# Four 5-tap recurrences on one core: both batches in one 512-column matmul, with lines and bias put into PSUM first

## What is computed

```python
def step(w, b):
    def f(carry, inp):
        nxt = inp + _conv1d(carry, w, b)     # 5 taps, 48 -> 48 channels, bias b
        return (nxt, nxt)
    return f
_, d_rest = lax.scan(step(down_w, down_b), d0, xs[1:])
...
_, u_rest = lax.scan(step(down_w, down_b), u0, seq)
...
_, r_rest = lax.scan(step(right_w, right_b), r0, ws[1:])
...
_, l_rest = lax.scan(step(left_w, left_b), l0, R[Ww - 2::-1])
```

## Time and profile before

| what | value |
|---|---|
| median of 3 runs | 10235.59 us |
| lowest, highest | 10228.61, 10245.71 us |
| span of the profiled execution | 10244.7 us |
| TensorE / VectorE / ScalarE / GpSimd busy in that span | 90% / 75% / 61% / 29% |
| the four ways, from the first hi matmul to the last | about 5097 to 9500 us of the span |

### The profile page before, as it was taken

The page is one execution under the profiler, slowest core; times in us unless marked ns, Lnnn a source line. Parts: engine busy times, 40 slices in busy tenths (PEclk is TensorE's granted clock), DMA queues, the critical chain, the costliest instruction groups (busy, mean ns, idle before and its releaser), DMA issues. The chain is left out here.

```text
span 10244.7 us, 212155 instructions
## 1 busy us (share of the span) xinstructions
PE 9248.3 (90%) x72264; PEld 8910.2 (87%) x72264; DVE 7669.6 (75%) x15539; ACT 6283.6 (61%) x11050; POOL 2991.7 (29%) x4335
## 2 busy tenths in 40 slices
PE   3999999999999999999899999999999999999100
PEld 3999999999999997777699999999999999999100
DVE  8888888777777775666677777777899987777323
ACT  3777777777777775444466668999633346666000
POOL 0000000000000000000166666666666666666000
PEclk9999999999999999999899999999999999999555
DMA  8888887666666666999889896777766657777999
GB/s 269 168 170 168 168 170 143 131 129 133 136 131 135 135 131 150 291 278 293 235 191 195 203 195 191 219 210 217 210 205 217 211 184 200 196 203 188 370 433 401
DMA packets 770603, 2101.31 MB, mean 205 GB/s; under 512 B 58976, under 2 KB 633728, under 8 KB 674256
## 3 DMA queue, kind: packets, MB, share of 16 engines
q1 hardware_dynamic: 629824, 1744.21, 66.6%
q0 software_dynamic: 34304, 151.01, 5.7%
q10 hardware_dynamic: 106368, 204.76, 5.6%
HBM read 1344.55 MB, written 754.97 MB: 205 GB/s over the span
## 5 line engine op out<-in xcount | busy, mean ns | idle before, releaser
L1542 ACT CAST hi<-rough 112x256 fp32r<-112x256 f32 x4096 | 1666.2, 407 | 1414.4 <-DVE rough L1455 1362.8
L1375 PE MATMUL scan_ps<-hi,scan_high 112*112 112x256 f32 x12264 | 2122.7, 282 | 30.7 <-ACT hi L1542 30.7
L1455 DVE SCALAR_TENSOR_TENSOR rough<-scan_ps,scan_bias,lines 112x256 f32<-112x256 f32 x4086 | 2136.4, 523 | 18.4 <-issue 14.0
L1386 PE MATMUL scan_ps_low<-lo,scan_high 112*112 112x256 f32 x12264 | 2136.1, 283 | 0.9 <-POOL lo L1487 0.7
L1381 PE MATMUL scan_ps_low<-hi,scan_low 112*112 112x256 f32 x12264 | 2123.9, 282 | 0.0
L463 PE MATMUL conv_ps<-tap_low,x_high 128*128 128x432 f32 (+2 forms) x6144 | 1905.4, 310 | 0.0
L463 PE MATMUL conv_ps<-tap_high,x_low 128*128 128x432 f32 (+2 forms) x6144 | 1904.0, 310 | 0.0
L463 PE MATMUL conv_ps<-tap_high,x_high 128*128 128x432 f32 (+2 forms) x6144 | 1882.0, 306 | 11.7 <-DVE x_edge L659 7.3
L1375 PEld LDWEIGHTS scan_ps<-hi,scan_high 112*112 112x112 f32 x12264 | 1695.0, 176 | 32.0 <-ACT hi L1542 31.5
L1386 PEld LDWEIGHTS scan_ps_low<-lo,scan_high 112*112 112x112 f32 x12264 | 1685.7, 176 | 6.3 <-POOL lo L1487 2.1
L1381 PEld LDWEIGHTS scan_ps_low<-hi,scan_low 112*112 112x112 f32 x12264 | 1684.1, 176 | 0.0
(11 more groups left out here) (142 smaller groups left out, 11625.5 us busy)
## 6 DMA issues: line engine op xcount, KB each, us to landing
raw<-x SPq DMA_DIRECT2D x764, 256.0 KB, 5.0
d_rows<-lines SPq DMA_DIRECT2D x32, 3584.0 KB, 30.4
u_cols<-lines SPq DMA_DIRECT2D x64, 1792.0 KB, 13.3
r_cols<-lines SPq DMA_DIRECT2D x32, 3584.0 KB, 24.3
lines<-u_cols SPq DMA_DIRECT2D x31, 3584.0 KB, 16.5
lines<-r_cols SPq DMA_DIRECT2D x30, 3584.0 KB, 16.6
lines<-d_rows SPq DMA_DIRECT2D x30, 3360.0 KB, 15.7
v_blocks<-xs ACTq DMA_DIRECT2D x128, 768.0 KB, 4.5
```

Source lines behind the costliest of these rows:

```text
L1375: last = nc.tensor.matmul(ps[:, b, 0:LP], high[:, shift], hi[:, b, (k - 1) % 2, shift:shift + LP], start=shift == 0, stop=shift == 2)
L1386: last = nc.tensor.matmul(ps_low[:, b, 0:LP], high[:, shift], lo[:, b, shift:shift + LP], start=False, stop=shift == 2)
L1455: nc.vector.scalar_tensor_tensor(rough[:, b, k % 2], ps[:, b, 0:LP], bias, line(way, s, k % T, b, kept), ALU.add, ALU.add).then_inc(rough_ ...
L1542: nc.scalar.copy(hi[:, b, k % 2, 1:LP + 1], rough[:, b, k % 2]).then_inc(hi_ready[b], 1)
```

## The change

Both batches go through one step together: every matmul, cast, subtraction and addition covers 2 x 256 columns. PSUM has four slots of one bank each, `ps[:, k % 4]`; a slot is first filled with the line of step k plus the bias ("seed"), and all nine products of step k are then added to it (`start=False`). `hi` is the slot rounded after the high products, `lo` = the full slot - `hi` (now on VectorE), and the state = `hi` + `lo` (now on GpSimd). The seeds are made by ScalarE in the down and right ways, with the normalisation folded in for down, and by VectorE in the up and left ways; each is issued `AHEAD` = 2 steps ahead, behind the step's own work of that engine. The separate normalisation and `rough` are gone. `hi` has 4 buffers and `lo` 2. ScalarE's copies of the ring come 2 steps later than before (`LAG`). SyncE's waits go by the count of seeds and states in place of `rough` and states.

TensorE issues the high products of step k+1 ahead of the low products of step k. The core of the diff:

```diff
+    LAG = 2
+    AHEAD = 2
+    HIS, LOS, SLOTS = 4, 2, 4
...
+        ps, gn_ps = psum("scan_ps"), ctx.enter_context(nc.psum_tensor("gn1_ps", [PP, 2, B], F32))
...
+        def slot_free(engine, way, g, k, kept):
+            if not (way == "down" and kept and k < SLOTS):
+                engine.wait_ge(lo_ready, states0(way) + T * g + k - SLOTS + 1)
+
+        def high_free(engine, way, g, k, first):
+            if not (way == "down" and first and k < HIS):
+                engine.wait_ge(state_done, states0(way) + T * g + k - HIS + 1)
...
 SyncE
-                    for b in range(B):
-                        sp.wait_ge(rough_ready[b], states0(way) + T * g - T)
+                    sp.wait_ge(seeded[way], seeds0(way) + T * g - T)
...
 TensorE
+                def high_products(way, g, k):
+                    pe.wait_ge(seeded[way], seeds0(way) + T * g + k + 1)
+                    pe.wait_ge(hi_ready, states0(way) + T * g + k)
+                    for shift in range(3):
+                        last = nc.tensor.matmul(slot(k), w_hi[:, TAPS_OF[way], shift], hi[:, (k - 1) % HIS, :, shift:shift + LP],
+                                                start=False, stop=False, skip_group_check=True)
+                    last.then_inc(conv_done, 1)
+
+                def low_products(way, g, k):
+                    pe.wait_ge(hi_ready, states0(way) + T * g + k + 1)
+                    for shift in range(3):
+                        nc.tensor.matmul(slot(k), w_lo[:, TAPS_OF[way], shift], hi[:, (k - 1) % HIS, :, shift:shift + LP],
+                                         start=False, stop=False, skip_group_check=True)
+                    pe.wait_ge(lo_ready, states0(way) + T * g + k)
+                    for shift in range(3):
+                        last = nc.tensor.matmul(slot(k), w_hi[:, TAPS_OF[way], shift], lo[:, (k - 1) % LOS, :, shift:shift + LP],
+                                                start=False, stop=shift == 2, skip_group_check=True)
+                    last.then_inc(low_done, 1)
+
+                def steps(way, g, first=False, last=False):
+                    for k in range(2 * T):
+                        if not (last and k == 2 * T - 1):
+                            high_products(way, g, k + 1)
+                        if not (first and k == 0):
+                            low_products(way, g, k)
...
 VectorE
+                def seed(way, g, s, k, kept=False, bare=False):
+                    arrived(v, way, g, s, k % T, kept)
+                    slot_free(v, way, g - s, k, kept)
+                    to, of = ps[:, k % SLOTS], line(way, s, k % T, kept)
+                    if bare:
+                        ins = nc.vector.tensor_copy(to, of)
+                    else:
+                        ins = nc.vector.tensor_scalar(to, of, b_sb[:, TAPS_OF[way]:TAPS_OF[way] + 1], None, ALU.add)
+                    ins.then_inc(dve_seeded, 1)
+
+                def steps(way, g, first=False, last=False):
+                    for k in range(2 * T):
+                        done = states0(way) + T * g + k
+                        v.wait_ge(hi_ready, done + 1)
+                        if not (first and k == 0):
+                            v.wait_ge(low_done, convs0(way) + T * g + k)
+                        if not (way == "down" and first and k < LOS):
+                            v.wait_ge(state_done, done - LOS + 1)
+                        nc.vector.tensor_tensor(low_of(k), ps[:, k % SLOTS], high_of(k), ALU.subtract).then_inc(lo_ready, 1)
+                        if way in laid:
+                            ahead = k + AHEAD
+                            if ahead < 2 * T:
+                                seed(way, g + ahead // T, ahead // T, ahead, first)
+                            elif not last:
+                                seed(way, g + ahead // T, ahead // T - 2, ahead - 2 * T)
...
 GpSimd
+                        room(way, g + s, s, k % T, kept)
+                        pool.wait_ge(hi_ready, states0(way) + T * g + k + 1)
+                        pool.wait_ge(lo_ready, states0(way) + T * g + k + 1)
+                        nc.gpsimd.tensor_tensor(state(way, s, k), high_of(k), low_of(k), ALU.add).then_inc(state_done, 1)
...
 ScalarE
+                def seed(way, g, s, k, kept=False, bare=False):
+                    arrived(act, way, g, s, k % T, kept)
+                    slot_free(act, way, g - s, k, kept)
+                    to, of = ps[:, k % SLOTS], line(way, s, k % T, kept)
+                    if way == "down":
+                        shift = gn1_bias if bare else down_shift
+                        for b in range(B):
+                            ins = nc.scalar.activation(to[:, b], of[:, b], ACT.Identity, bias=shift[:, b:b + 1], scale=gn1_scale[:, b:b + 1])
+                    elif bare:
+                        ins = nc.scalar.copy(to, of)
+                    else:
+                        ins = nc.scalar.activation(to, of, ACT.Identity, bias=b_sb[:, TAPS_OF[way]:TAPS_OF[way] + 1], scale=1.0)
+                    ins.then_inc(act_seeded, 1)
...
+                        high_free(act, way, g, k, first)
+                        nc.scalar.copy(high_of(k), ps[:, k % SLOTS]).then_inc(hi_ready, 1)
+                        if way in laid:
+                            if not (first and k < LEAD + LAG):
+                                behind(way, g, k)
+                        else:
+                            ahead = k + AHEAD
+                            if ahead < 2 * T:
+                                seed(way, g + ahead // T, ahead // T, ahead, first)
+                            elif not last:
+                                seed(way, g + ahead // T, ahead // T - 2, ahead - 2 * T)
```

More of the change, by code:

```diff
@@ L1366, in _ @@
             def _(pe):
[L1367 to L1388, removed]
@@ L1393, in _ @@
                 nc.tensor.matmul(gn_ps[:, 1, 0:B], g112_sb[:], var[:], start=True, stop=True).then_inc(group_var, 1)
+                pe.wait_ge(edges_clear, 1)
+                for j in range(SLOTS):
+                    nc.tensor.matmul(slot(j), w_hi[:, 0, 0], hi[:, 0, :, 0:LP], start=True, stop=False, skip_group_check=True
+                                     ).then_inc(slots_set, 1)
                 for way in WAYS:
-                    steps(way, 0, 1)
-                    with pe.Fori(1, G // 2) as i:
-                        steps(way, 2 * i, 0)
+                    steps(way, 0, first=True)
+                    with pe.Fori(1, G // 2 - 1) as i:
+                        steps(way, 2 * i)
+                    steps(way, G - 2, last=True)
             @block.vector
@@ L1419, in _ @@
                 inverse_root(nc, link, gn1_scale[:], var[:], root[:])
[L1420 to L1430, removed]
+                link(nc.vector.scalar_tensor_tensor(gn1_bias[:], gm[:], -1.0, gn1_scale[:], ALU.mult, ALU.mult))
@@ L1432, in room, with _ @@
+                for way in WAYS:
+                    if way in laid:
+                        v.wait_ge(state_done, states0(way))
+                        for k in range(AHEAD):
+                            seed(way, 0, 0, k, True, k == 0)
+                    steps(way, 0, first=True)
+                    with v.Fori(1, G // 2 - 1) as i:
+                        steps(way, 2 * i)
+                    steps(way, G - 2, last=True)
+            @block.gpsimd
+            def _(pool):
                 def room(way, g, s, k, kept):
@@ L1440, in room @@
                         elif way == "right":
[L1441 to L1447, removed]
-                        s = k // T
[L1449 to L1477, removed]
@@ L1479, in _ @@
[L1479 to L1488 removed]
+                            pool.wait_ge(stored["up"][s], 16 * STORES["up"] * (G // 2))
@@ L1492, in _ @@
                 pool.wait_ge(between_clear, 2)
[L1493 removed]
                 for way in WAYS:
[L1495 to L1498 removed]
+                    steps(way, 0, True)
+                    with pool.Fori(1, G // 2) as i:
                         steps(way, 2 * i)
```

123 lines of the change are left out of this document (57 added, 66 removed).

## The result

The changed kernel takes 12,972.15 us (median of 4 runs, 12,965.31 to 12,977.67) against 10,237.12 us: a ratio of 1.267, 95% interval 1.265 to 1.269. It is slower, as forecast, but by 2735 us and not by 1545; the time lies above the range, between the forecast and the rival in which the clock falls. All times in the experiments but that of the kernel with the seed first are of single runs; in each of these the granted clock of the down and right ways was 1.00, so a lower one in up and left is not put down to the slower kind of execution, in which the kernel before once took 12,312.85 us at a mean clock of 0.72.

The account below looks back on a forecast made before the run. It took TensorE as the bound. Down and right save 89 us, up and left add 1626 waiting for VectorE's seed, way ends add 8: +1545, forecast 11,780 us; own range 11,500 to 11,950, with two rivals 11,480 to 12,340.

Parts of the forecast that it names:

- the rival in which the clock falls: Up and left: TensorE's per-step wait drops the granted clock to 0.50; 13,710 us in all; chance 0.10.
- The two rows between which it chose: Way starts: up waited 1.35 and 0.24 us, clock stayed 1.00; left waited 1.46 and 0.50, clock went to 0.50.
- the slow step: Up and left at clock 0.50: a step of 5.62 us, with 0.427 us per 512-column matmul.
- The cause of the wait: Up and left: high(k+2) waits for VectorE's seed, issued behind `lo`(k); TensorE idles about 1.6 us a step.
- The rival in which the seeds are ahead after all: Up and left: seed is in PSUM when low(k) ends, TensorE bounds all four ways; 10,066 us; chance 0.07.
- A step at full clock: Up and left at clock 1.00: 3.73 us a step against 2.139, adding 1626 us over 1022 steps.
- The seed at the rate of PSUM: VectorE's seed in up and left: 0.73 us, between bounds of 0.48 (copy within SBUF) and 1.27 (beside GpSimd).
- GpSimd did not hold it up: Rival for up and left: GpSimd's addition stretches VectorE's seed to 1.27 us; 12,330 us in all; chance 0.05.
- Down and right: TensorE stays the bound without idle time; steps of 2.052 us against 2.139, saving 89 us over 1022 steps.
- ScalarE's list: Down and right: cast 0.62 us plus seed, some 1.8 us a step; 2.44 at the upper ends in down.
- The mis-sized term: TensorE's 512-column matmul: 0.2133 us of columns plus 0.015 lost, 0.228 us each, nine a step.
- the loss between matmuls: TensorE: 0.012 us lost at 256 columns, 0.015 at 432; taken to stay with each matmul while their number halves.

## Why the prediction was wrong

The step that failed is the choice in the rival on the clock: "Here nine of 512 columns stand in 3.73 us, which is nearer to the first (19 of 256 in 3 us), so I keep 1.00." The two rows between which it chose were single events, two waits each, and the new step fell about halfway between them. It was then counted as all or nothing, 0.72 against 0.10, while the kernel goes back and forth: a few of the loop's steps run at full clock (3.9 us), some at half (up to 5.8 us), and most change within the step, 4.95 us on the mean of the loop in up. The prediction had 5.62 for the slow step, and its terms for it hold (a slow first group is 1.62 for 1.48 us, 0.14 more, as it had); the mean of 4.84, with the written-out steps in it, lies between the two. A range that held this would have needed a case between them. The Trainium skill (TensorE: Matmul & The Clock Gate, A second HAM failure mode) describes such a going back and forth, in a kernel that cycles through PSUM banks, and the trace here agrees that the clock moves between two levels: 0.70 on the mean, out of 1.00 and 0.50. I read it as support for a rival, and then gave that rival the price of a clock that stays down.

Point by point:

- **The cause of the wait: right.** High(k+2) waits for VectorE's seed, 1.50 to 1.58 us a step (1.6 forecast); turning two blocks of VectorE's program round takes it all away. The rival in which the seeds are ahead after all is what that kernel does: 10,175 us, where the rival had 10,066.
- **A step at full clock: 3.85 us for 3.73.** The eight matmuls are 1.87 for 1.82. From the start of the last low matmul to the low part it is 0.49 for 0.42 (6203.97 to 6204.93, less two of 0.234). The low part is 0.69 as forecast, the next instruction 0.61 after its start for 0.62, the seed 0.745 for 0.73, VectorE to TensorE 0.06 for 0.05, and the slower first group 0.09 as forecast (0.95 in place of 0.86). In the loop VectorE to TensorE is 0.07 more.
- **The seed at the rate of PSUM: right**; 0.745 us, and 0.684 without the bias, is near neither bound. GpSimd did not hold it up: it ran at the same time in every step.
- **Down and right: TensorE bound, but the gain was smaller.** A step is 2.108 us for 2.052, so 32 us came back in place of 89. ScalarE's list is 0.59 for the cast and 1.06 or 1.16 for the seed, inside the bounds. The mis-sized term is the matmul, 0.234 for 0.228. I took the loss between matmuls as a fixed amount from four starts. It is 12 ns at 256 columns, 14 at 336 (the filler, 0.154 us), 17 at 432 (the median over many, 0.197 us, where the four in the earlier trace rows gave 0.195) and 21 at 512: it grows with the columns. The Trainium skill's rule for isolated matmuls (TensorE: Matmul & The Clock Gate, Back-to-back issue gap), 0.216 us at 512, is further off still.
- **The error in all**: 12,972 - 11,780 = 1192 us is 1022 x (4.84 - 3.73) = 1134 for up and left, and 1022 x 0.056 = 57 for down and right. Of the 1134, the kernels with a filled wait show some 940 to be the clock; the rest is the step at full clock, 0.12 us longer than forecast and 0.07 more in the loop.

The version to keep is the one with the seed first, 10,175 us: 0.54% under the kernel before. It has what the change could give: 2044 steps at 2.11 in place of 2.14 us.

## What to carry to other kernels

Where work is made "two steps ahead", count the distance on the engine that consumes it, along both programs: if the producer's instruction stands behind a wait for the consumer's instruction just before the one that needs it, the distance is nil. When TensorE gets a wait in every step of a long loop, treat the clock as a term of the sum with a mean between its two levels, and settle it by measuring; a wait at the edge costs or saves 1000 us here for 0.06 us of work. If such a wait can't be moved, putting spare matmuls in it is a cheap test of whether the clock is the cost.

## What was not expected of the hardware

- At waits of 1.51 and 1.57 us a step, with the same nine matmuls between, the granted clock in the up way was 1.00 and 0.70, and steps 3.87 and 4.94 us (1600/414 and 2000/405).
- One matmul of 336 columns in a wait of 1.57 us kept the clock at 1.00, and did as much as nine of them.
- Of two waits ahead of TensorE's high products, one was long satisfied. With the seed's wait ahead of it TensorE started 0.06 us after the seed in written-out steps and 0.14 in the loop; with the seed's wait behind it, 0.15 and 0.05.
